# A decoder layer on one core: the causal mask taken off TensorE and done by GpSimd and VectorE

## The reference

```python
Q = jnp.einsum('bsd,hkd->bhsk', x, WQ)      # K, V in the same way
scores = jnp.einsum('bhqd,bhkd->bhqk', Q, K) / math.sqrt(d_k)
causal = jnp.tril(jnp.ones((seq_len, seq_len), dtype=bool))
scores = jnp.where(causal, scores, -jnp.inf)
probs = jax.nn.softmax(scores, axis=-1)
attn = jnp.einsum('bhqk,bhkv->bhqv', probs, V)
x = _layernorm(x + jnp.einsum('bhsv,hdv->bsd', attn, WO))
x = _layernorm(x + xattn(x, ctx, mask)); x = _layernorm(x + moe(x))
```

## Time and profile before

| | |
|---|---|
| Time before, median of 3 runs | 788.39 us (785.49 to 791.27) |
| The profiled execution's own time | 791.14 us, its span 789.3 us |
| TensorE busy | 741.0 us (94%) |
| VectorE busy | 554.9 us (70%) |
| ScalarE busy | 380.1 us (48%) |
| GpSimd busy | 280.2 us (35%) |
| Granted TensorE clock, mean | 0.983 |

### The profile page before, as it was taken

The page is one execution under the profiler, slowest core; times in us unless marked ns, Lnnn a source line. Parts: engine busy times, 40 slices in busy tenths (PEclk is TensorE's granted clock), DMA queues, the critical chain, the costliest instruction groups (busy, mean ns, idle before and its releaser), DMA issues.

```text
span 789.3 us, 12650 instructions
## 1 busy us (share of the span) xinstructions
PE 741.0 (94%) x4632; PEld 496.5 (63%) x4632; DVE 554.9 (70%) x1195; ACT 380.1 (48%) x639; POOL 280.2 (35%) x285
## 2 busy tenths in 40 slices
PE   6688999999999998988999998999999999999994
PEld 3345443444444432554777787877888888888883
DVE  1287867768768670495778744699778768777777
ACT  2222666566566667323444434654444544544441
POOL 8323001240321315222113213574545545545542
PEclk9989999999999999999999978999999999999999
DMA  4865951523515000170000000000000000000000
GB/s 151 168 163 153 247 113 29 85 56 43 96 25 76 18 15 19 44 312 0 2 1 1 2 1 1 0 2 1 1 1 15 14 1 1 27 1 2 7 21 27
DMA packets 21316, 38.29 MB, mean 49 GB/s; under 512 B 5768, under 2 KB 9320, under 8 KB 20872
## 3 DMA queue, kind: packets, MB, share of 16 engines
q1 hardware_dynamic: 19688, 35.32, 19.0%
q0 software_dynamic: 1568, 2.18, 1.2%
HBM read 28.64 MB, written 8.65 MB: 47 GB/s over the span
## 4 chain that ended last, share of the span: by engine, by line
PE 72%; DVE 14%; issue 4%; ACT 3%; DMA 3%; POOL 2%; SPq 1%; POOLq 0%; DVEq 0%; ACTq 0%
PE ps L1118 19%; PE ps L1216 10%; PE ps L1014 9%; PE ps L990 8%; PE ps L972 7%; PE ps L1155 3%; PE ps L1136 3%; DVE neg_max L700 3%; DVE x_tok L875 3%; PE ps L1170 2%; PE ps L1145 2%; PE ps L977 2%; PE ps L993 2%; POOL stacks L429 1%; DMA stacks<-m_rows 1%
## 5 line engine op out<-in xcount | busy, mean ns | idle before, releaser
L700 DVE TENSOR_REDUCE neg_max<-ps 128x1 f32<-128x512 f32 (+3 forms) x304 | 180.6, 654 | 63.3 <-PE ps L977 50.2
L1118 PE MATMUL ps<-x_split,w_split 128*128 128x512 f32 x816 | 204.5, 400 | 0.7 <-POOL w_split L510 0.5
L584 ACT ACTIVATE temps<-ps 128x1024 f32<-128x1024 f32 (+1 forms) x192 | 148.9, 811 | 93.0 <-PE ps L993 68.3
L1118 PEld LDWEIGHTS ps<-x_split,w_split 128*128 128x128 f32 x816 | 152.0, 192 | 32.2 <-issue 1.4
L510 POOL TENSOR_TENSOR w_split<-stacks,w_split 128x512 fp32r<-128x512 f32 x70 | 90.5, 1292 | 129.5 <-ACT w_split L617 129.5
L972 PE MATMUL ps<-stacks 96*128 96x512 bf16 (+3 forms) x384 | 104.8, 331 | 13.3 <-DMA stacks<-qk_parts 7.3
L1216 PE MATMUL ps<-w_split,h_split 128*128 128x256 f32 x816 | 110.5, 285 | 6.5 <-DVE x_tok L875 5.2
L1216 PEld LDWEIGHTS ps<-w_split,h_split 128*128 128x128 f32 x816 | 106.4, 190 | 15.2 <-issue 10.6
L875 DVE SCALAR_TENSOR_TENSOR x_tok<-ps,o_norm,x_tok 128x256 f32<-128x256 f32 x256 | 105.5, 474 | 0.1
L990 PE MATMUL ps<-stacks 99*128 99x512 bf16 (+3 forms) x384 | 99.4, 328 | 2.9 <-DMA stacks<-m_rows 1.6
L623 ACT ACTIVATE temps<-ps 128x512 f32<-128x512 f32 x68 | 40.6, 597 | 112.7 <-PE ps L1118 112.6
(11 more groups left out here) (120 smaller groups left out, 888.6 us busy)
## 6 DMA issues: line engine op xcount, KB each, us to landing
stacks<-qk_parts SPq DMA_DIRECT2D x96, 128.0 KB, 5.5
qk_parts<-temps SPq DMA_DIRECT2D x8, 768.0 KB, 4.1
stacks<-in_w SPq DMA_DIRECT2D x1, 4352.0 KB, 13.9
stacks<-in_w SPq DMA_DIRECT2D x1, 2176.0 KB, 18.6
x_T<-in_xT SPq DMA_DIRECT2D x4, 512.0 KB, 7.6
x_tok<-in_x SPq DMA_DIRECT2D x1, 2048.0 KB, 12.5
out_tokens<-x_tok SPq DMA_DIRECT2D x16, 128.0 KB, 1.7
temps<-row_sums POOLq DMA_DIRECT2D x28, 64.0 KB, 2.5
```

What stands on the lines that cost most here:

```text
L584: nc.scalar.activation(pt[:, n % 4, :, 0:w], ps[:, 2 + 2 * (n % 2):4 + 2 * (n % 2), 0:w], ACT.Exp, scale=SCALE).then_inc(b_exp, 1)
L700: nc.vector.tensor_reduce(nmx[:, c, h0:h0 + nh, i], ps[:, A_BANKS[n % 3], 0:w * nh].rearrange("p (h k) -> p h k", h=nh), axis=AX.X, op=ALU ...
L1118: last = nc.tensor.matmul(ps[:, 2 * part + e % 2, :], w13s[:, split_buf(e), wp, k, P * part:P * part + P], xs[:, bass.ds(c, 1), xp, k, :], ...
```

## The change

- TensorE's 512 mask matmuls are gone, and with them `causB`.
- B side: the exponentials of the 16 diagonal B jobs of a group (`DIAG`) now come out unmasked. GpSimd sets those on the wrong side of the diagonal to zero, in place, with one `affine_select` a job over 2 x 128 columns (`cut`). A product of a diagonal block waits for it (`b_cut`).
- A side: the reduction of a diagonal job leaves out the last 128 columns of each head (`lead`). These are taken by a `tensor_tensor_reduce` for each head, which adds `causA` (now float32 in SBUF) to the scores in PSUM, writes the sum back to PSUM and the negated maximum to a third plane of `nmx`. Step M has one more instruction that joins this plane.
- Row sums: all their transfers go to SyncE's queue (`sums`), one group later; GpSimd multiplies two groups later (`normalise(g - 2)`), between the cuts of the first and of the second half.

```diff
@@ -72,6 +72,8 @@
 C0 = CH // P
+DIAG = [n for n, (c, j, _) in enumerate(B_JOBS) if P * j >= CH * c]
+ND = len(DIAG)
@@ -205,14 +207,13 @@
         identb = sb("ident_b", [P, P], BF16)
-        causA = sb("caus_a", [P, P], BF16)
-        causB = sb("caus_b", [P, P], BF16)
+        causA = sb("caus_a", [P, P], F32)
...
-        nmx = sb("neg_max", [P, NC, HG, TB], F32)
+        nmx = sb("neg_max", [P, NC + 1, HG, TB], F32)
...
@@ -366,6 +369,27 @@
+            def sums(g):
+                base = 48 * g
+                sp.wait_ge(o_kept, 2 * g + 2)
+                sp.dma_start(l_dram[0, g], on[DH * (1 - g % 2):P:HS, g, :]).then_inc(l_moved, 16)
+                sp.wait_ge(l_moved, base + 16)
+                sp.dma_start(lsum[:, g % 3, :], l_dram[0, g].rearrange("h (x n) -> (h x) n", n=HG * S // P))\
+                  .then_inc(l_moved, 16)
+                sp.wait_ge(l_recip, g + 1)
+                sp.dma_start(l_dram[1, g].rearrange("h (x n) -> (h x) n", n=HG * S // P), lrec[:, g % 3, :])\
+                  .then_inc(l_moved, 16)
+                sp.wait_ge(l_moved, base + 48)
+                if g == 0:
+                    sp.wait_ge(filled, 8)
+                if g >= 2:
+                    sp.wait_ge(o_scaled, g - 1)
+                for h in range(HG):
+                    at = HS * h + DH * (g % 2)
+                    sp.dma_start(rl[at:at + DH, g % 2, :],
+                                 l_dram[1, g, h].unsqueeze(0).to_broadcast([DH, S])).then_inc(l_spread[g % 2], 16)
@@ -397,25 +421,13 @@
+                if g >= 1:
+                    sums(g - 1)
+            sums(NG - 1)
...
-            g = NG - 1
-            sp.wait_ge(o_kept, 2 * NG)
-            sp.dma_start(l_dram[0, g], on[0:P:HS, g, :]).then_inc(l_last, 16)
...
-            sp.wait_ge(l_last, 16 * 7)
+            sp.wait_ge(b_cut, ND * NG)
@@ -453,46 +465,37 @@
-            def sums_out(g):
-                pool.wait_ge(o_kept, 2 * g + 2)
-                base = 16 * 7 * g
-                pool.dma_start(l_dram[0, g], on[DH * (1 - g % 2):P:HS, g, :]).then_inc(l_moved, 16)
-                pool.wait_ge(l_moved, base + 16)
-                pool.dma_start(lsum[:, g % 3, :], l_dram[0, g].rearrange("h (x n) -> (h x) n", n=HG * S // P))\
-                  .then_inc(l_moved, 16)
+            zero = nc.gpsimd.to_reg(0.0)
+            def cut(g, n):
+                pool.wait_ge(b_exp, g * NB + n + 1)
+                diag = pt[:, n % 4, :, 0:P]
+                nc.gpsimd.affine_select(diag, diag, [[0, 2], [1, P]], ALU.is_ge, zero, base=0,
+                                        channel_multiplier=-1).then_inc(b_cut, 1)
...
-                base = 16 * 7 * g
-                pool.wait_ge(l_recip, g + 1)
-                pool.dma_start(l_dram[1, g].rearrange("h (x n) -> (h x) n", n=HG * S // P), lrec[:, g % 3, :])\
-                  .then_inc(l_moved, 16)
-                pool.wait_ge(l_moved, base + 48)
-                if g >= 2:
-                    pool.wait_ge(o_scaled, g - 1)
-                for h in range(HG):
-                    at = HS * h + DH * (g % 2)
-                    pool.dma_start(rl[at:at + DH, g % 2, :],
-                                   l_dram[1, g, h].unsqueeze(0).to_broadcast([DH, S])).then_inc(l_moved, 16)
-                pool.wait_ge(l_moved, base + 112)
+                pool.wait_ge(l_spread[g % 2], 64 * (g // 2 + 1))
...
-                if g + 3 < NG:
-                    pool.wait_ge(pv_done, NV * (g + 1))
-                    n = g + 3
+                for n in DIAG[:2 * C0]:
+                    cut(g, n)
+                if 1 <= g < NG - 2:
+                    n = g + 2
+                    pool.wait_ge(pv_done, NV * g)
...
-                if g == NG - 1:
-                    break
-                sums_out(g)
-                normalise(g)
+                if g >= 2:
+                    normalise(g - 2)
+                for n in DIAG[2 * C0:]:
+                    cut(g, n)
+            normalise(NG - 2)
@@ -696,27 +699,39 @@
...
-                        nc.vector.tensor_reduce(nmx[:, c, h0:h0 + nh, i],
-                                                ps[:, A_BANKS[n % 3], 0:w * nh].rearrange("p (h k) -> p h k", h=nh),
-                                                axis=AX.X, op=ALU.max, negate=True).then_inc(a_max, 1)
...
+                        scores = ps[:, A_BANKS[n % 3], 0:w * nh].rearrange("p (h k) -> p h k", h=nh)
+                        diag = P * (i + 1) <= CH * (c + 1)
+                        lead = w - P if diag else w
+                        if lead:
+                            last = nc.vector.tensor_reduce(nmx[:, c, h0:h0 + nh, i], scores[:, :, 0:lead],
+                                                           axis=AX.X, op=ALU.max, negate=True)
+                        if diag:
+                            for s in range(nh):
+                                h = h0 + s
+                                last = nc.vector.tensor_tensor_reduce(
+                                    scores[:, s, lead:w], scores[:, s, lead:w], causA[:], scale=-1.0, scalar=3e38,
+                                    op0=ALU.add, op1=ALU.min, accum_out=nmx[:, NC, h, i:i + 1])
+                        last.then_inc(a_max, 1)
                     if kind == "R":
...
-                        flat = [nmx[:, c].rearrange("p h i -> p (h i)") for c in range(NC)]
...
+                        flat = [nmx[:, c].rearrange("p h i -> p (h i)") for c in range(NC + 1)]
...
+                        nc.vector.tensor_tensor(nm[:, 0, :], nm[:, 0, :], flat[2], ALU.min).then_inc(m_chain, 1)
...
@@ -967,15 +982,11 @@
                         wait(pe, a_max, (g + 1) * NA + (n - 1 if n < 2 else n - 2))
-                        diag = P * (i + 1) <= CH * (c + 1)
                         for s in range(nh):
...
                                                     ks[0:KR, ua, h0 + s, CH * c:CH * c + w],
-                                                    start=True, stop=not diag)
-                            if diag:
-                                last = nc.tensor.matmul(ps[:, A_BANKS[n % 3], w * (s + 1) - P:w * (s + 1)], identb[:], causA[:],
-                                                        start=False, stop=True)
+                                                    start=True, stop=True)
                         last.then_inc(a_ready, 1)
@@ -984,13 +995,10 @@
                         wait(pe, b_exp, g * NB + n - 1)
-                        diag = P * j >= CH * c
                         for s in range(2):
...
                             last = nc.tensor.matmul(ps[:, bank, 0:w], ks[0:KM, u, 2 * pr + s, P * j:P * j + P],
-                                                    qs[0:KM, u, 2 * pr + s, q0:q0 + w], start=True, stop=not diag)
-                            if diag:
-                                last = nc.tensor.matmul(ps[:, bank, 0:P], identb[:], causB[:], start=False, stop=True)
+                                                    qs[0:KM, u, 2 * pr + s, q0:q0 + w], start=True, stop=True)
                         last.then_inc(b_ready, 1)
@@ -1008,6 +1016,8 @@
                 pe.wait_ge(b_exp, base * 2 + (2 * p + 2))
+                if 2 * p in DIAG:
+                    pe.wait_ge(b_cut, base // NV * ND + DIAG.index(2 * p) + 2)
                 if j == 0:
```

More of the change, by code:

```diff
@@ L256, in build @@
             sem(n) for n in ("a_ready", "a_max", "m_chain", "m_cut", "m_T", "m_row"))
+        b_cut = sem("b_cut")
+        l_spread = [sem(f"l_spread{u}") for u in range(2)]
         b_ready, b_exp, pv_done, o_kept, l_moved, l_recip, o_done, vg_ready = (
@@ L359, in _ @@
             load_x(3)
-            for dst, name in ((identb, "identb"), (causA, "causA"), (causB, "causB")):
+            for dst, name in ((identb, "identb"), (causA, "causA")):
                 sp.dma_start(dst[:], a[name]).then_inc(ld_caus, 16)
@@ L698, in group @@
                         if n == 0:
-                            wait(dve, m_chain, (g + 1) * 4)
-                        nc.vector.tensor_reduce(nmx[:, c, h0:h0 + nh, i],
-                                                ps[:, A_BANKS[n % 3], 0:w * nh].rearrange("p (h k) -> p h k", h=nh),
-                                                axis=AX.X, op=ALU.max, negate=True).then_inc(a_max, 1)
+                            wait(dve, m_chain, (g + 1) * 5)
+                        scores = ps[:, A_BANKS[n % 3], 0:w * nh].rearrange("p (h k) -> p h k", h=nh)
[11 more added lines that the diff above has]
+                        last.then_inc(a_max, 1)
                     if kind == "R":
@@ L1276 @@
     data["identb"] = (row == col).astype(bf)
-    data["causA"] = np.where(col > row, NEG, 0.0).astype(bf)
-    data["causB"] = np.where(row > col, NEG, 0.0).astype(bf)
+    data["causA"] = np.where(col > row, NEG, 0.0).astype(np.float32)
     data["hm"] = (row // DH == np.arange(8)[None, :]).astype(np.float32)
```

31 lines of the change are left out of this document (10 added, 21 removed).

## The result

| | us |
|---|---|
| before, median of 4 runs | 789.83 (785.49 to 791.31) |
| after, median of 4 runs | 805.28 (804.78 to 805.44) |
| ratio | 1.0192, 95% interval 1.0157 to 1.0226 |
| forecast | 827 (806 to 856), that is +38.9 |
| own time of the two profiled executions | 791.14 and 805.42, spans 789.3 and 803.7 |

A forecast was written before the change was run, and what follows sets the result against it. VectorE's reductions were taken to bound the attention sections: +51.3 us VectorE work, -14.8 idle time, +1.4 tails, +1 last group, together +38.9 on the median 788.4, so 827 us, range 806 to 856.

The forecast's parts named there:

- the section: Attention group's stretch of VectorE reductions, 25.81 us, with 22.59 of reductions; the tail of 5.7 us follows it.
- The idle time left in a full-clock section: VectorE's idle time in a section, 2.9 us before, forecast to fall to 1.0 (ends: 0 and 2.9).
- the pair: Two VectorE instructions of one masked reduction, main half and one-column second half; taken at 0.33 us, bounds 0.29 to 0.44.
- 32 x 0.33 = 10.56: VectorE, per set of 38 jobs: 32 added masked reductions at 0.33 us each, 10.56 us.
- the lower bound of 0.29: Least price of a masked reduction's two instructions on VectorE, short of both fixed parts vanishing: 0.29 us.
- The first half's own lower bound, 0.206: VectorE's main half on 128 PSUM columns: 0.286 us less 0.08 for overlapping neighbours, so at least 0.206.
- the forecast's own formula: Whole kernel's change in terms of a masked reduction's price p: 256 p - 45.6 us.
- In the section and in the prologue VectorE covers them: TensorE's masks, 31 us in all, were claimed to count only in the tail and in the last group.
- 1.9 gives way: Each of 7 attention groups' sections loses 1.9 us of VectorE's 2.9 idle: -13.3 us.
- The prologue's section: The stretch before the groups, 30.50 us with VectorE busy for 27.53; forecast at 30.5 + 4.9 us.
- No change: Rival for the whole kernel: p from 0.15 to 0.21, or 0.25 with all idle used; 781 to 796 us; chance 0.06.
- the rivals named: Relief of TensorE shows (faster, 0.04), no change (0.06), cuts bound the group (858 us, 0.10), late sums (862 us, 0.02).

The follow-up runs named there:

- the A side alone: Kernel before with the change's masked reductions, third plane and step M on VectorE, B jobs' mask matmuls left on TensorE: 799.8 us, ratio 1.0101.
- B side alone: Changed kernel with the A side of the kernel before (mask matmuls, plain reductions); GpSimd's cuts and SyncE's transfers kept: 785.75 us, ratio 0.9925.
- A masks alone: Kernel before without the mask matmuls of the A jobs, nothing else changed: 779.0 us, ratio 0.9853.
- both: Changed kernel with no A-side mask and plain reductions over whole jobs, GpSimd's cuts kept on the B side: 777.08 us, ratio 0.9831.

## Why the forecast missed

**Right.** VectorE bounds the section in the main; the masked reductions make the kernel slower; the relief of TensorE doesn't pay for it. The cuts count at product 10 and in the last group only. The transfers on SyncE's queue cost nothing that shows. The idle time left in a full-clock section was forecast as 1.0 us; it is about 1.2 (26.54 busy in the group, less some 1.25 of step M, in a section of 26.5).

**Wrong: the price of the pair.** The term "32 x 0.33 = 10.56", and the lower bound of 0.29 under it. The rows:

```profile
81.53 0.14 DVE L712 DVE_READ_ACCUMULATOR2_ANT neg_max<- 128x1 f32 x1
81.53 0.33 DVE L712 CUSTOM_DVE_ANT_0 ps<-ps,caus_a 128x128 f32<-128x128 f32 x1
81.78 0.14 DVE L712 DVE_READ_ACCUMULATOR2_ANT neg_max<- 128x1 f32 x1
81.78 0.33 DVE L712 CUSTOM_DVE_ANT_0 ps<-ps,caus_a 128x128 f32<-128x128 f32 x1
...
83.86 0.42 DVE L707 TENSOR_REDUCE neg_max<-ps 128x1 f32<-128x256 f32 x1
84.20 0.28 DVE L712 CUSTOM_DVE_ANT_0 ps<-ps,caus_a 128x128 f32<-128x128 f32 x1
84.41 0.14 DVE L712 DVE_READ_ACCUMULATOR2_ANT neg_max<- 128x1 f32 x1
84.41 0.42 DVE L707 TENSOR_REDUCE neg_max<-ps 128x1 f32<-128x256 f32 x1
```

A masked reduction that stands behind a plain one takes 0.21 us from start to start (84.20 to 84.41), one that stands behind another masked one 0.25 (81.53 to 81.78). The second half, on which I put at least 84 ns, starts in the very moment in which the next instruction starts. Ahead of another masked reduction it costs these 0.04 us, ahead of a plain one next to nothing (128 x 384: 470 ns from start to start, 465 in the kernel before):

```profile
L712 DVE CUSTOM_DVE_ANT_0 ps<-ps,caus_a 128x128 f32<-128x128 f32 x256 | 70.8, 302 | 35.6 <-PE ps L986 35.6
...
L712 DVE DVE_READ_ACCUMULATOR2_ANT neg_max<- 128x1 f32 x256 | 36.1, 141 | 0.0
```

141 ns is what its row lasts, not what it costs. My two bounds each added the second half's row to the first half's, after I had read from the earlier trace rows that neighbours overlap, and applied it to the first half alone. The first half's own lower bound, 0.206, is what was measured. The mean price follows from a full-clock group: 26.54 - 23.71 us of busy time, less 0.22 for step M, is 2.61; with the 4.36 removed, 6.97 over 32 heads is **0.22 us**. The starts give the same: 22 of a group's 32 stand behind another kind of instruction (0.206 us) and 10 behind a masked reduction (0.249). By the forecast's own formula 256 x 0.22 - 45.6 = +10.7 us. A group at full clock grew by 0.78, where that formula has 2.8 - 1.9 + 0.2 = 1.1. So the sum was sound, its largest entry half as large again as it should be.

**Wrong: the clock was not in the sum.** The earlier trace rows has a granted clock of 1.00 for the group and the last group and 0.94 for the prologue; the sum took all of them as they were, though the prediction also said that TensorE would wait more. It stood neither among the rivals nor among what could make the forecast wrong. In the profiled execution it is 11 us. The rest of the change (prologue, full-clock sections, tails, last group) is 3.2 + 4.9 + 0.7 - 0.5 = 8.3 us, near the 10.7 of the formula, though half-clock time is in the prologue's 3.2 as well, and 5 us were given back behind the attention. So that the median came within 5 us of the formula is in part luck: 11 us of spells and 5 given back are in neither. The trace shows no long gap on TensorE, but many short ones, most of them waits for VectorE. From 115 to 300 us of the changed kernel (us in total, times, longest):

```profile
PE ps L986 <- DVE neg_max L712: 9.4, 20, 0.8
PE ps L1008 <- DVE m_parts L735: 5.5, 5, 1.1
PE ps L1024 <- ACT temps L587: 1.4, 5, 0.3
PE ps L986 <- DVE neg_max L707: 0.9, 6, 0.2
```

(The third line is product 10, which waits for the cuts, as shown above.) In the kernel before the same stretch has one wait of 1.1 us. The sum of the waits doesn't decide it, though: the A side alone waits 11.4 us for VectorE there and has no spell in it. What the runs show is that zeros in place of the missing matmuls end the spells, and that the same matmuls in groups of 29.95 us have none; the rule behind both isn't shown. The Trainium skill (TensorE: Matmul & The Clock Gate, A second HAM failure mode: psum-queue depth-cycling) tells of another kernel in which brief and frequent idling between groups of matmuls makes the clock swing between its two levels; the spells here, and their end with the zeros, agree with it.

**Wrong in its reason: "In the section and in the prologue VectorE covers them".** Taking the masks away with VectorE's work unchanged shortens a section by 0.6 us (B side alone), 1.0 (A masks alone) and 1.5 (both). The 2.9 us of idle time in a section were in part TensorE's mask time. That the idle time left came out as forecast (1.2 against 1.0) is then in part luck: "1.9 gives way" took in the same microseconds for another reason.

**Small.** A cut at 410 ns instead of 740: tails +0.1 instead of +0.2, last group -0.5 instead of +1.

**Luck.** The prologue's section, forecast at 30.5 + 4.9 us, took 35.4. With a pair at 0.22 its growth would have been 2.8 - 1.5 = 1.3; the rest goes with the clock as far as the runs tell, 0.83 granted in it against 0.94 (in the A side alone it took 33.6 at 0.88). The section began 1.2 us sooner, which is why group 0 begins only 3.2 us later.

**The rivals.** "No change" was priced at p from 0.15 to 0.21; with 0.22 the pair alone stands at its edge. With the first half's lower bound for the whole pair the formula gives 788.4 + 256 x 0.206 - 45.6 = 795.5 us, so a range that reached down to there would have held the result. None of the rivals named took place.

## What to carry to other kernels

Ask first whether an operation is needed before asking which engine does it cheapest: a softmax's maximum needs no mask. Leaving the A side's out of the kernel before gave 1.5% where moving it to VectorE cost 1.0%; with the B side's mask moved to GpSimd as well, it was a gain of 1.7% against a loss of 1.9%. Where a group of instructions is priced, subtract starts from starts, for both halves of an instruction pair; the length of a row is no price. When work is taken off TensorE and another engine holds the pace, look at the granted clock as a term of its own: here the same matmuls kept the full clock in groups of 29.9 us and lost it in five of seven at 32.3 and more.

## What the runs showed of the hardware

- A `tensor_tensor_reduce` on 128 columns of PSUM: 302 ns for its row, 0.21 us from start to start behind a plain reduction and 0.25 behind another of its kind. Its accumulator read (a row of 141 ns) starts together with the next instruction and costs 0.04 us or less.
- GpSimd's `affine_select` in place on 128 x 256 float32: 410 ns, little more than half of its two-input operation on the same size (736 ns). Product 10, which waits for it, starts 0.14 to 0.15 us after its end.
- Half-clock spells of TensorE of about 7 us, each 2.5 us of the attention in four groups of the changed kernel. All went when zeros were multiplied at the places of the removed work, all but one and a half when it was at half of them. What decides in which of several equal groups one falls stays open: groups 1 and 4 of the changed kernel had none, and the rows ahead of a spell and ahead of its absence read alike.
- One execution of 1825 us with doubled TensorE rows and unchanged VectorE rows at a granted clock that read 1.00; its cause is not known.
